# Row-tiled scores, joined latent weights and one shared order of work in a two-layer attention and feed-forward kernel

## The chip, the core and the metric

The kernel runs on one core of one Trainium2 chip. A core has TensorE (PE, matmuls), VectorE (DVE), ScalarE (ACT), GpSimd (POOL) and a queue for transfers (SP). Each engine takes its own instructions strictly in the order in which they are written, and semaphores join the engines. The metric is the device time of one execution in microseconds (us).

## The reference

Thirty-two entries of 128 tokens by 128 channels pass through two layers, each an attention and a feed-forward part, in float32:

```python
x = x + L0_xattn(ctx, layernorm(x), keep_mask, ...)   # 8 heads of 64, keys = context (120) and x (128)
x = x + L0_ffn(layernorm(x), Wm, Wp, Wc1, Wc2)        # iterated with a routed mask
x = x + L1_xattn(layernorm(x), ctx, ctx, mask, ...)   # 16 heads of 8, keys = context (120)
x = x + L1_ffn(layernorm(x), ...)                     # latent attention (16 heads of 8), then 8 experts
```

In the first attention q and k are divided by their own norms, the masked softmax runs over 248 keys, and the projected result is layer-normalized before it is added to x. In the latent attention of the last part the keys and values come from a narrow product:

```python
c = h @ Wdkv                     # 128 x 64
k = (c @ Wuk).reshape(B, S, HEADS, hd)
v = (c @ Wuv).reshape(B, S, HEADS, hd)
```

## The kernel before

x stays in the core's memory (SBUF) for the whole program. The stages run one after another, with a barrier between them: `l0_attention`, `l0_ffn` with `route`, `attention16` for L1 (names with `l_`), `attention16` for the latent attention (`mla_`), and `moe`.

**First attention.** The order of each engine is written out by hand in its `body(n)`, one entry n per turn, in `run_entries`; work of entry n+1 and n+2 is mixed in. Two units u of four heads each share the softmax. For entry n+2 the chain is: `norm_inputs` (DVE, L650, L652), `turn_inputs` (PE), `make_kvT` (ACT), three projections q, kc and kl (PE, L481, L482, L487) with their copies `qk` (ACT), squares `sq` (ACT, L591), `sum_squares` (DVE, L657 and L662 into `ssm`), and on POOL `norm_qk`: a power on 24 columns into `r_norm` (L742) and a product on 1536 columns into `qkn` (L745). In the next turn PE turns `qkn` (L494, L498, L504), ACT and DVE copy it to `KT` and `QZ`, and `scores` follows. A head has 64 rows of q; `QZ` holds each head's q in its own half of 128 rows with zeros in the other half, so that a score matmul (L384) uses all 128 rows. The key mask is added by a bfloat16 matmul per bank (L380). Softmax: `dve_max` (L162), exponentials (ACT, L171), `invert_sums` (DVE: L177, then L414 which copies the inverses wide into `r_wide`), transposes of the probabilities (L184, L190), their copies (ACT L196, DVE L201), `turn_sums` (L421), `multiply_v` (L436, L438), `scale_out` (L447) and `project` (L453). `y_moments` (L675 to L687) takes six small DVE instructions from the statistics of the projected row to its variance; POOL raises it to a power (L751), DVE normalizes (L692), POOL weighs and adds to x.

**The two 16-head attentions** have an order each (`body_l1`, `body_mla`), in turns by `run_steps`. PE writes the masks (L1431, 32 by 32 tiles) and the scores (L1436, four row tiles of 32) of an entry into four banks; DVE takes two maxima (L1558, L1565), the first for half the heads that ACT exponentiates with a bias (L1524), the second for the half that DVE shifts (L1574) and ACT exponentiates at once (L1531). Four groups of transposed probabilities (L1446) are copied by ACT or DVE (L1380) and multiplied with V and with ones in column tiles (L1456, L1459). The latent attention first projects to 64 columns (L1405), copies that on ACT (L1510), and takes keys and values from it (L1418, L1419).

## Time and profile before

| What | us |
|---|---|
| median of 3 runs (1519.94 to 1520.65) | 1520.29 |
| the profiled execution itself | 1520.62 |
| its span, first to last instruction | 1518.9 |
| PE busy | 1320.3 (87%) |
| DVE busy | 1031.7 (68%) |
| ACT busy | 759.3 (50%) |
| POOL busy | 559.6 (37%) |

The span is the time from the first to the last instruction of the program; some 1.7 us lie around it. In that execution the first attention works from 26 to 579 us, the first feed-forward part and its routing to 744, the L1 attention to 1010, the latent attention from 1042 to 1268, and the experts from 1277 to the end. A matmul of float32 is recorded as two passes, so that a count of 2 in a row is one matmul; its end is modelled, and the distance from one start to the next tells more than its duration. "PEclk" is the clock of PE that was granted, as a share of 2.4 GHz.

A window's row gives its bounds and length, then for PE, its weight loads (PEld), DVE, ACT and POOL the busy time and the number of instructions, then PEclk and what the DMA engines did. A timeline's row gives start, duration, engine, line, operation, output and input, the tile in TensorE as rows*columns, the shape, the count, and in brackets the idle time before it and what ended it.

### The profile page before, as it was taken

Reading aid. Unit: us, or ns where it says so; the run is one execution under the profiler, and the core shown is the slowest. Engines: PE = TensorE matmul, PEld = TensorE weight load, DVE = VectorE, ACT = ScalarE, POOL = GpSimd, SP = SyncE. Lnnn points to the kernel's source line nnn. Section 1 sums busy time; section 2 is a strip of 40 time slices with the busy share of each in tenths; the row PEclk is TensorE's granted clock in tenths of the full one; section 3 lists DMA queues with packets and bytes.
Section 4 is the critical chain, followed back from the end, with each engine's and each line's share of the span. In section 5 each row is a group of like instructions: output and inputs, shape, how many; then the busy total and the mean of one; then the engine's idle time right before and its main releaser. Section 6 shows DMA issues by size and latency. Waiting matters only on the chain. (4 is left out here: it accounts for less than half of the span.)

```text
span 1518.9 us, 38140 instructions
## 1 busy us (share of the span) xinstructions
PE 1320.3 (87%) x13781; PEld 963.8 (63%) x13781; DVE 1031.7 (68%) x2266; ACT 759.3 (50%) x2067; POOL 559.6 (37%) x546
## 2 busy tenths in 40 slices
PE   1699999999999996931389988969999997999998
PEld 0377676776776773421277676747878885777776
DVE  5377777777777773767388888868999995343432
ACT  1467767767767661300155555536666663333332
POOL 3556555555555543000221222234222222334333
PEclk9899999999999997965599999988999998999999
DMA  7000000000000000000000000010000000000000
GB/s 200 0 1 0 0 0 0 0 0 0 0 0 0 0 1 0 0 1 0 9 11 7 8 8 8 7 57 2 1 0 0 0 2 1 8 8 14 7 7 14
DMA packets 22727, 14.56 MB, mean 10 GB/s; under 512 B 6377, under 2 KB 21609, under 8 KB 22538
## 3 DMA queue, kind: packets, MB, share of 16 engines
q1 hardware_dynamic: 22520, 13.75, 3.5%
q8 instruction: 37, 0.61, 0.2%
q14 instruction: 24, 0.20, 0.0%
q10 hardware_dynamic: 146, 0.01, 0.0%
HBM read 11.66 MB, written 2.10 MB: 9 GB/s over the span
## 5 line engine op out<-in xcount | busy, mean ns | idle before, releaser
L742 POOL TENSOR_TENSOR r_norm<-ssm,mhalf 128x24 f32<-128x24 f32 x32 | 133.6, 4176 | 176.1 <-DVE ssm L662 176.1
L171 ACT ACTIVATE l_probs<-psum,l_n_max 128x248 f32<-128x248 f32 x256 | 117.0, 481 | 101.4 <-DVE l_n_max L162 101.4
L1845 ACT ACTIVATE hid<-psum 128x512 f32<-128x512 f32 x128 | 76.3, 597 | 136.3 <-PE psum L1793 136.3
L1906 DVE TENSOR_TENSOR prod<-psum,combine 128x512 f32<-128x512 f32 x64 | 44.2, 691 | 143.9 <-PE psum L1803 143.9
L1803 PEld LDWEIGHTS psum<-w,hid 128*128 128x128 f32 x1024 | 123.1, 192 | 26.8 <-issue 26.8
L1937 POOL TENSOR_TENSOR acc<-acc,prod 128x512 f32<-128x512 f32 x64 | 81.1, 1268 | 146.9 <-DVE prod L1906 146.9
L384 PE MATMUL psum<-KT,QZ 128*128 128x248 f32 x512 | 128.4, 373 | 0.0
L1803 PE MATMUL psum<-w,hid 128*128 128x128 f32 x1024 | 123.4, 275 | 0.0
L1793 PE MATMUL psum<-moe_hT,w 128*128 128x512 f32 x256 | 122.0, 605 | 0.0
L384 PEld LDWEIGHTS psum<-KT,QZ 128*128 128x128 f32 x512 | 98.1, 192 | 18.9 <-issue 0.7
L1658 POOL TENSOR_TENSOR l_QX<-l_qT,l_own_slots 128x512 f32<-128x512 f32 x32 | 33.3, 1040 | 185.1 <-ACT l_qT L1504 178.5
L745 POOL TENSOR_TENSOR qkn<-qk,r_norm 128x1536 f32<-128x1536 f32 x32 | 88.4, 2762 | 3.6 <-POOL r_norm L742 2.2
L1658 POOL TENSOR_TENSOR mla_QX<-mla_qT,mla_own_slots 128x512 f32<-128x512 f32 x32 | 33.3, 1040 | 149.5 <-ACT mla_qT L1504 149.5
L1380 ACT COPY l_probsT<-psum 120x512 f32<-120x512 f32 x64 | 37.5, 585 | 100.4 <-PE psum L1446 100.4
L162 DVE TENSOR_REDUCE l_n_max<-psum 128x4 f32<-128x992 f32 x64 | 75.7, 1183 | 8.8 <-PE psum L384 8.8
L1446 PE MATMUL psum<-ident,mla_probs 128*128 128x128 f32 x512 | 76.2, 283 | 1.5 <-ACT mla_probs L1524 1.3
L657 DVE TENSOR_REDUCE ss<-sq 128x24 f32<-128x1536 f32 x32 | 56.1, 1753 | 30.1 <-ACT sq L591 30.1
L1524 ACT ACTIVATE mla_probs<-psum,mla_n_max 128x128 f32<-128x128 f32 x256 | 69.5, 382 | 13.9 <-DVE mla_n_max L1558 13.9
L201 DVE COPY l_probsT<-psum 128x512 f32<-128x512 f32 x64 | 43.9, 685 | 41.6 <-PE psum L190 41.6
L1446 PE MATMUL psum<-ident,l_probs 128*120 128x128 f32 x512 | 70.5, 281 | 0.0
L1524 ACT ACTIVATE l_probs<-psum,l_n_max 128x120 f32<-128x120 f32 x256 | 68.0, 385 | 5.0 <-DVE l_n_max L1558 5.0
L586 ACT COPY qk<-psum 128x512 f32<-128x512 f32 (+1 forms) x96 | 54.5, 619 | 30.6 <-PE psum L487 22.7
(307 smaller groups left out, 3458.8 us busy)
## 6 DMA issues: line engine op xcount, KB each, us to landing
X<-x_in SPq DMA_DIRECT2D x8, 256.0 KB, 4.9
out_dram<-acc SPq DMA_DIRECT2D x32, 64.0 KB, 1.5
CT<-ctx_in SPq DMA_DIRECT2D x8, 240.0 KB, 6.2
l_cT<-ctxT_in SPq DMA_DIRECT2D x32, 60.0 KB, 1.8
w<-w_in SPq DMA_DIRECT2D x1, 1024.0 KB, 4.9
wm<-wm_in SPq DMA_DIRECT2D x1, 768.0 KB, 4.6
wp<-wp_in SPq DMA_DIRECT2D x1, 768.0 KB, 6.7
wkv<-wkv_in SPq DMA_DIRECT2D x1, 512.0 KB, 5.1
```

What stands on the lines that cost most here:

```text
L162: dve.tensor_reduce(n_max[u][:, :].rearrange("p (c j) -> p c j", c=2), psum[:, 2 * u:2 * u + 2, 0:HB * K].rearrange("p c (j k) -> p c j k" ...
L171: e = act.activation(probs[u][:, h, :], psum[:, 2 * u + h // HB, (h % HB) * K:(h % HB + 1) * K], ACT.Exp, bias=n_max[u][:, h:h + 1], accum ...
L384: mm = pe.matmul(psum[:, 2 * u + c, j * K:(j + 1) * K], QZ[par][:, h, :], KT[par][:, h // 2, :], start=False, stop=True, skip_group_check= ...
L742: pool.tensor_tensor(r_norm[:, :], ssm[:, :], mhalf[:, 0:3 * H], ALU.pow).then_inc(s["norm_inverted"], 1)
L745: pool.tensor_tensor(qkn[:, :, :].rearrange("p a (h d) -> p (a h) d", d=HD), qk[:, :, :].rearrange("p a (h d) -> p (a h) d", d=HD), r_norm ...
L1446: tr = pe.transpose(psum[0:K, 4 + g % 2, j * P:(j + 1) * P], probs[par][:, 4 * g + j, :], ident[:, :])
L1524: e = act.activation(probs[par][:, h, :], psum[:, h // 4, (h % 4) * K:(h % 4 + 1) * K], ACT.Exp, bias=n_max[par][:, h:h + 1])
L1658: pool.tensor_tensor(QX[par][:, :, :], qT[:, :].unsqueeze(1).broadcast_to([P, 4, P]), own_slots[:, :].unsqueeze(2).broadcast_to([P, 4, P]) ...
L1793: pe.matmul(psum[:, 2 + i % BANKS, :], w1[:, e, half * P:(half + 1) * P], hT[par][:, :], start=True, stop=True).then_inc(hidden[i], 1)
L1803: mm = pe.matmul(psum[:, 5 + e % 2, b * D:(b + 1) * D], hid[i % RING][:, b * P:(b + 1) * P], w2[:, i, :], start=(half == 0), stop=(half == ...
L1845: act.activation(hid[i % RING][:, :], psum[:, 2 + i % BANKS, :], ACT.Silu).then_inc(activated[i], 1)
L1937: pool.tensor_tensor(a[:, :, :], a[:, :, :], prod[e % 2][:, :, :], ALU.add).then_inc(summed[e], 1)
```

## The change

It has four parts.

1. **Row tiles in the first attention.** `QT` holds q without zeros, two heads in the two halves of 128 rows. A score matmul takes 64 rows, and the two heads of a pair stand next to each other in the order, each with its own bank. The mask is added by matmuls of 64 rows likewise, from `keep_now`, which POOL copies for each entry; the mask row is made twice at the start, in rows 0 and 64. `multiply_v` alternates between its two column tiles.
2. **Aggregate moments.** `bn_aggr` and one addition replace the six instructions between `y_stat` and `y_var`.
3. **Joined latent weights.** Once, at the start of the latent attention, PE forms Wdkv Wuk and Wdkv Wuv (`joined`). Keys and values then come straight from `zT`; L1405, the copy L1510 and the waits on it go.
4. **Orders.** The first attention gets a new order on every engine and now uses `run_steps`, which also does its first and last entries. Both 16-head attentions share one new `body` on every engine.

```diff
+        joined = sb("joined", [D, 2, D])
+                    pe.transpose(psum[0:LAT, 6, 0:D], wdkv[:, :], ident[:, :]).then_inc(w_turned, 1)
+                    pe.wait_ge(w_copied, 1)
+                    pe.matmul(psum[:, 7, 0:D], wdkvT[:, :], wk[:, :], start=True, stop=True)
+                    pe.matmul(psum[:, 7, D:2 * D], wdkvT[:, :], wv[:, :], start=True, stop=True).then_inc(w_joined, 1)
...
-            pe.matmul(psum[:, 2 * u + c, 0:2 * K], first_row[:, :], keep_row[:, entries(n), :].broadcast_to([P, 2, K]),
-                      start=True, stop=False, skip_group_check=True)
-            for j in range(2):
-                h = 4 * u + 2 * c + j
-                mm = pe.matmul(psum[:, 2 * u + c, j * K:(j + 1) * K], QZ[par][:, h, :], KT[par][:, h // 2, :],
-                               start=False, stop=True, skip_group_check=True)
+                        for r in range(2):
+                            pe.matmul(psum[:, 2 * u + r, 0:2 * K], first_row[64 * r:64 * r + 64, :],
+                                      keep_now[par][64 * r:64 * r + 64, :].unsqueeze(1).broadcast_to([64, 2, K]),
+                                      start=True, stop=False, skip_group_check=True)
+                        for j in range(2):
+                            for r in range(2):
+                                mm = pe.matmul(psum[:, 2 * u + r, j * K:(j + 1) * K], QT[par][64 * r:64 * r + 64, 2 * u + j, :],
+                                               KT[par][64 * r:64 * r + 64, 2 * u + j, :], start=False, stop=True,
+                                               skip_group_check=True)
...
+                for r in (0, 64):
+                    dve.tensor_scalar(keep_row[r:r + 1, :, 0:C], keep8[r:r + 1, :].rearrange("a (b c) -> a b c", b=B), 1.0, -NEG_MAX,
+                                      ALU.subtract, ALU.mult)
...
-                    dve.tensor_tensor(y_sums[:, :], y_stat[:, 1:3], y_stat[:, 4:6], ALU.add)
-                    dve.tensor_tensor(y_diff[:, :], y_stat[:, 1:2], y_stat[:, 4:5], ALU.subtract).then_inc(s["y_aggr"], 1)
...
+                        dve.bn_aggr(y_moment[:, :], y_stat[:, :]).then_inc(s["y_aggr"], 1)
+                        wait(dve, s["y_aggr"], n + 1)
+                        wait(dve, s["y_inverted"], n)
+                        dve.tensor_scalar(y_var[:, :], y_moment[:, 1:2], LN_EPS, None, ALU.add).then_inc(s["y_var_ready"], 1)
...
+                def body(n, par):
+                    values_x(n + 1)
+                    scores(n, 1, par)
+                    project(n - 1)
+                    turn_inputs(n + 2)
+                    turn_probs0(n, 0)
+                    turn_probs1(n, 0)
+                    project_kc(n + 2)
+                    turn_sums(n, 0)
+                    project_q(n + 2)
+                    multiply_v(n, 0, par)
+                    turn_probs0(n, 1)
+                    turn_kc(n + 1)
+                    project_kl(n + 2)
+                    turn_probs1(n, 1)
+                    turn_kl(n + 1)
+                    turn_q(n + 1)
+                    multiply_v(n, 1, par)
+                    turn_sums(n, 1)
+                    values_c(n + 2)
+                    scores(n + 1, 0, 1 - par)
...
+                def body(n, par):
+                    norm_inputs(n + 2)
+                    maximum(n, 1)
+                    invert_sums(n, 0)
+                    y_moments(n - 1)
+                    copy_pt1(n, 0)
+                    scale_out(n, 0)
+                    invert_sums(n, 1)
+                    copy_pt1(n, 1)
+                    copy_kl(n + 1, 1 - par)
+                    copy_qT(n + 1, 1 - par)
+                    sum_squares(n + 2)
+                    y_normalize(n - 1)
+                    maximum(n + 1, 0)
+                    scale_out(n, 1)
+                    x_moments(n - 2)
...
+                def body(n, par):
+                    weigh(n - 2)
+                    copy_keep(n + 2, par)
+                    invert_deviation(n - 1)
+                    add_to_x(n - 2)
+                    invert_norms(n + 2)
+                    norm_qk(n + 2)
+                    later_scales(n)
...
+                def body(n, par):
+                    copy_q(n + 1)
+                    copy_group(act.copy, act, n - 1, 2)
+                    copy_k(n + 1, 1 - par)
+                    exp_b(n, par)
+                    copy_group(act.copy, act, n, 0)
+                    exp_a(n + 1, 1 - par)
...
+                def body(n, par):
+                    copy_input(dve, n + 1)
+                    copy_group(dve.tensor_copy, dve, n - 1, 3)
+                    add_projection(n - 2)
+                    max_b(n, par)
+                    take_stats(n - 2)
+                    shift_b(n, par)
+                    copy_group(dve.tensor_copy, dve, n, 1)
+                    copy_values(dve.tensor_copy, dve, n + 1, 1 - par)
+                    invert_sums(n - 1)
+                    scale_out(n - 1)
+                    max_a(n + 1, 1 - par)
```

The first place is DVE in a turn of the first attention. Before, from the wide copy of the inverses for unit 0 (`r_wide0`) to the scaled output; `l0_n_max1` is the maximum of unit 1:

```order
L177 RECIPROCAL l0_r_sums0<-l0_sums0 128x4
L414 COPY r_wide0<-l0_r_sums0 128x256
L162 TENSOR_REDUCE l0_n_max1<-psum 128x4
L201 COPY l0_probsT0<-psum 128x512
L675 BN_STATS y_stat<-y 128x6
L678 TENSOR_TENSOR y_sums<-y_stat 128x2
L679 TENSOR_TENSOR y_diff<-y_stat 128x1
L681 TENSOR_SCALAR y_mean<-y_sums 128x1
L682 TENSOR_SCALAR y_within<-y_sums 128x1
L683 SCALAR_TENSOR_TENSOR y_between<-y_diff 128x1
L687 TENSOR_TENSOR y_var<-y_within,y_between 128x1
L447 TENSOR_TENSOR outT<-psum,r_spread 128x256
```

The same place after the change:

```order
L577 TENSOR_SCALAR ln_c<-CT,mean_c,rstd_c 120x128
L607 TENSOR_REDUCE l_n_max1<-psum 128x4
L615 RECIPROCAL l_r_sums0<-l_sums0 128x4
L618 COPY r_wide0<-l_r_sums0 128x256
L640 BN_STATS y_stat<-y 128x6
L642 BN_AGGR y_moment<-y_stat 128x2
L645 TENSOR_SCALAR y_var<-y_moment 128x1
L626 COPY l_probsT0<-psum 128x512
L634 TENSOR_TENSOR outT<-psum,r_spread 128x256
```

The maximum now stands ahead of the wide copy, and the moments of y ahead of the copy of the probabilities instead of behind it.

The second place is PE in the first attention, from the end of `multiply_v` of unit 1 to `project` (L453 before, L444 after). Before:

```order
L380 MATMUL psum<-keep_row,first_row 128x496
L384 MATMUL psum<-KT,QZ 128x248 x2
L380 MATMUL psum<-keep_row,first_row 128x496
L384 MATMUL psum<-KT,QZ 128x248 x2
L380 MATMUL psum<-keep_row,first_row 128x496
L384 MATMUL psum<-KT,QZ 128x248 x2
L380 MATMUL psum<-keep_row,first_row 128x496
L384 MATMUL psum<-KT,QZ 128x248 x2
L453 MATMUL psum<-wo,outT 128x128 x4
```

After:

```order
L420 MATMUL psum<-ident,r_wide 128x128 x2
L368 MATMUL psum<-wkv,kvT 120x512
L386 MATMUL psum<-keep_now,first_row 128x496 x2
L391 MATMUL psum<-KT,QT 128x248 x4
L375 MATMUL psum<-wkv,kvT 128x512
L386 MATMUL psum<-keep_now,first_row 128x496 x2
L391 MATMUL psum<-KT,QT 128x248 x4
L444 MATMUL psum<-wo,outT 128x128 x4
```

The number of score and mask matmuls is the same (eight and four); the two value projections now stand ahead of each unit's scores.

The third place is PE in the L1 attention, one turn. Before, from one `project` (L1466) to the next transposes (L1446):

```order
L1466 MATMUL psum<-l_wo,l_outT 128x128
L1431 MATMUL psum<-l_bias,ident_bf 32x480 x16
L1436 MATMUL psum<-l_kT,l_QX 128x120 x16
L1446 MATMUL psum<-ident,l_probs 120x128 x8
L1456 MATMUL psum<-l_probsT,l_V 32x128 x4
L1459 MATMUL psum<-l_probsT,l_ONE 32x128 x4
L1456 MATMUL psum<-l_probsT,l_V 32x128 x4
L1459 MATMUL psum<-l_probsT,l_ONE 32x128 x4
L1399 MATMUL psum<-ident,l_zn 128x128
L1406 MATMUL psum<-l_zT,l_wq 128x128
L1418 MATMUL psum<-l_cT,l_wk 128x120
L1419 MATMUL psum<-l_wv,l_cT 120x128
```

After, from the scores (L1386) to the second half of V (L1406):

```order
L1386 MATMUL psum<-l_kT,l_QX 128x120 x16
L1396 MATMUL psum<-ident,l_probs 120x128 x8
L1358 MATMUL psum<-ident,l_zn 128x128
L1416 MATMUL psum<-l_wo,l_outT 128x128
L1396 MATMUL psum<-ident,l_probs 120x128 x4
L1365 MATMUL psum<-l_zT,l_wq 128x128
L1367 MATMUL psum<-l_cT,l_wk 128x120
L1368 MATMUL psum<-l_wv,l_cT 120x128
L1406 MATMUL psum<-l_probsT,l_V 32x128 x4
L1409 MATMUL psum<-l_probsT,l_ONE 32x128 x4
L1406 MATMUL psum<-l_probsT,l_V 32x128 x4
L1409 MATMUL psum<-l_probsT,l_ONE 32x128 x4
```

The input's transpose is now separated from the projection that needs its copy by eight to twelve other passes, `project` is a turn later, and the groups of transposes lie between other work.

## Rows read from the trace of the kernel before

**Rows 1.** Windows: one turn each of the first, the L1 and the latent attention.

```profile
324.10:340.30 16.20, 16.18 (x106) 11.48 (x105) 11.99 (x26) 11.21 (x32) 8.88 (x7) 1.00 0.00 0
861.20:869.20 8.00, 7.15 (x138) 5.58 (x138) 6.66 (x12) 4.54 (x13) 1.80 (x3) 1.00 0.03 8
1137.20:1144.60 7.40, 7.40 (x147) 5.90 (x141) 6.92 (x10) 4.74 (x16) 2.19 (x4) 1.00 0.00 0
```

**Rows 2.** Timeline of PE in a turn of the first attention: start, duration, instruction.

```profile
324.98 1.02 PE L462 MATMUL psum<-wkv,kvT 128*120 128x512 f32 x2
325.84 0.60 PE L184 MATMUL psum<-ident,l_probs 128*120 128x128 f32 x4
326.27 0.60 PE L190 MATMUL psum<-ident,l_probs 128*128 128x128 f32 x4
...
335.00 0.45 PE L436 MATMUL psum<-l_probsT,VC 120*64 120x128 f32 x4
...
336.08 0.38 PE L380 MATMUL psum<-keep_row,first_row 128*128 x1
336.30 1.00 PE L384 MATMUL psum<-KT,QZ 128*128 128x248 f32 x4
337.14 0.37 PE L380 MATMUL psum<-keep_row,first_row 128*128 x1
```

**Rows 3.** Timeline of PE in a turn of the L1 attention, then of the latent attention.

```profile
861.49 0.42 PE L1431 MATMUL psum<-l_bias,ident_bf 32*32 32x480 bf16 x16
...
862.94 1.09 PE L1446 MATMUL psum<-ident,l_probs 128*120 128x128 f32 x8
863.96 0.43 PE L1456 MATMUL psum<-l_probsT,l_V 120*32 120x128 f32 x8
...
864.97 0.33 PE L1399 MATMUL psum<-ident,l_zn 128*128 128x128 f32 x1
...
1138.73 0.43 PE L1405 MATMUL psum<-mla_zT,mla_wdkv 128*64 128x128 f32 x2
1139.10 0.49 PE L1406 MATMUL psum<-mla_zT,mla_wq 128*128 128x128 f32 x2
...
1141.40 0.66 PE L1446 MATMUL psum<-ident,mla_probs 128*128 128x128 f32 x4
1141.99 0.48 PE L1418 MATMUL psum<-mla_latT,mla_wk 64*128 64x128 f32 x2
```

**Rows 4.** Timeline of DVE in the first attention, second half of the same turn.

```profile
333.26 0.69 DVE L201 COPY l_probsT<-psum 128x512 f32<-128x512 f32 x1 [1.33 <-PE psum L190]
334.15 0.76 DVE L372 TENSOR_SCALAR QZ<-psum,qk_scale 64x512 f32<-64x512 f32 x1 [0.21 <-PE psum L498]
...
336.59 1.75 DVE L657 TENSOR_REDUCE ss<-sq 128x24 f32<-128x1536 f32 x1 [0.47 <-ACT sq L591]
338.38 0.18 DVE L662 TENSOR_SCALAR ssm<-ss 128x24 f32<-128x24 f32 x1
338.46 1.18 DVE L162 TENSOR_REDUCE l_n_max<-psum 128x4 f32<-128x992 f32 x1
```

**Rows 5.** Timelines of POOL and of DVE: what stood beside `qkn`.

```profile
322.45 4.18 POOL L742 TENSOR_TENSOR r_norm<-ssm,mhalf 128x24 f32<-128x24 f32 x1 [5.00 <-DVE ssm L662]
326.79 2.76 POOL L745 TENSOR_TENSOR qkn<-qk,r_norm 128x1536 f32<-128x1536 f32 x1 [0.16 <-POOL r_norm L742]
...
338.63 4.17 POOL L742 TENSOR_TENSOR r_norm<-ssm,mhalf 128x24 f32<-128x24 f32 x1 [5.00 <-DVE ssm L662]
...
327.87 1.69 DVE L678 TENSOR_TENSOR y_sums<-y_stat 128x2 f32<-128x2 f32 x1
...
69.28 2.76 POOL L745 TENSOR_TENSOR qkn<-qk,r_norm 128x1536 f32<-128x1536 f32 x1
...
69.40 2.79 DVE L414 COPY r_wide<-l_r_sums 128x256 f32<-128x256 f32 x1
```

**Rows 6.** Timeline of DVE ahead of the first attention.

```profile
21.13 2.14 DVE L331 TENSOR_SCALAR keep_row<-keep 1x3840 bf16<-1x3840 uint8 x1
```

More of the change, by code:

```diff
@@ L206, in run_entries, with run_steps @@
-def run_entries(eng, body, before_loop=None):
-    body(0, 0, first=True)
-    if before_loop:
-        before_loop()
-    with eng.Fori(0, B // 2 - 2) as i:
-        body(2 * i + 1, 1)
-        body(2 * i + 2, 0)
-    body(B - 3, 1)
-    body(B - 2, 0, after=False)
-    body(B - 1, 1, after=False, next_=False)
+def run_steps(eng, body):
+    for n in range(-2, 4):
+        body(n, n % 2)
+    with eng.Fori(0, B // 2 - 4) as i:
+        body(2 * i + 4, 0)
+        body(2 * i + 5, 1)
+    for n in range(B - 4, B + 2):
+        body(n, n % 2)
@@ L458, in _, with turn_inputs, project_kc @@
             def _(pe):
+                def turn_inputs(m):
+                    if there(m):
+                        wait(pe, s["ln_made"], m + 1)
+                        wait(pe, s["vc_copied"], m)
+                        pe.transpose(psum[:, 6, 0:C], ln_c[0:C, :], ident[0:C, 0:C])
+                        pe.transpose(psum[:, 6, P:2 * P], ln_x[:, :], ident[:, :]).then_inc(s["ln_turned"], 1)
+                def project_kc(m):
+                    if there(m):
+                        wait(pe, s["kvT_made"], m + 1)
+                        pe.matmul(psum[0:C, 6, :], kvT[:, 0:C], wkv[:, 0:INNER], start=True, stop=True).then_inc(s["kc_proj"], 1)
@@ L459, in values_c, with turn_kl @@
+                def turn_kl(m):
+                    if there(m):
+                        wait(pe, s["kcT_copied"], m + 1)
+                        for c in range(4):
+                            tr = pe.transpose(psum[:, 6, c * P:(c + 1) * P], qkn[:, 2, c * P:(c + 1) * P], ident[:, :])
+                        tr.then_inc(s["klT_turned"], 1)
                 def values_c(m):
-                    wait(pe, s["klT_copied"], m)
-                    pe.matmul(psum[0:C, 6, :], kvT[:, 0:C], wkv[:, INNER:], start=True, stop=True).then_inc(s["vc_proj"], 1)
+                    if there(m):
+                        wait(pe, s["klT_copied"], m)
+                        wait(pe, s["kc_copied"], m + 1)
+                        pe.matmul(psum[0:C, 6, :], kvT[:, 0:C], wkv[:, INNER:], start=True, stop=True).then_inc(s["vc_proj"], 1)
@@ new lines, in project @@
+                def project(n):
+                    if there(n):
+                        wait(pe, out_scaled[1], n + 1)
+                        for c in range(4):
+                            mm = pe.matmul(psum[:, 5, 0:D], outT[:, c, :], wo[:, c, :], start=(c == 0), stop=(c == 3))
+                        mm.then_inc(s["projected"], 1)
+                def body(n, par):
[19 more added lines that the diff above has]
+                    scores(n + 1, 0, 1 - par)
@@ L561, in _ @@
+                run_steps(pe, body)
             @block.scalar
@@ L585, in copy_qk, with copy_part @@
+                def copy_part(m, part, proj, copied, bank, rows):
+                    if there(m):
+                        wait(act, s["normed"], m)
                         wait(act, s[proj], m + 1)
-                        act.copy(qk[0:rows, i, :], psum[0:rows, bank, :]).then_inc(s[copied], 1)
+                        act.copy(qk[0:rows, part, :], psum[0:rows, bank, :]).then_inc(s[copied], 1)
                 def square_qk(m):
-                    wait(act, s["kl_copied"], m + 1)
-                    wait(act, s["ss_summed"], m)
```

827 lines of the change are left out of this document (329 added, 498 removed).

## The prediction

> **What bounds the kernel now.** I read the time spent by stage first, then the windows of one turn, then the timelines of PE, DVE and POOL within a turn. The reader should see in the windows that PE is busy in 16.18 of 16.20 us of a turn of the first attention, at the full clock, with DVE at 11.99, ACT at 11.21 and POOL at 8.88 [rows 1]. So the first attention, 553 of the 1518.9 us (26 to 579), is bound by PE, and what is taken from PE counts until another chain is longer. In the L1 attention PE has 7.15 of 8.00 us and DVE 6.66, and no engine is full: there the order sets the turn. The latent attention has PE at 7.40 of 7.40 and DVE at 6.92 [rows 1]; PE first, and DVE closely behind.
>
> From start to start PE needs 0.86 us for a matmul of 512 columns in its two passes, 0.43 to 0.44 for four transposes (0.109 each), 0.84 for four score passes of 248 columns (0.21 each), 0.22 for the mask of a bank, and 1.08 for `multiply_v` of a unit, from its first L436 to the mask behind it [rows 2].
>
> **First attention on PE.** Before, eight heads take 16 score passes and four masks: 16 × 0.21 + 4 × 0.22 = 4.2 us. After, a score matmul uses 64 rows, and two heads stand in the two halves of the array with separate banks. If the halves work side by side, eight pairs of passes remain, 8 × 0.209 = 1.67, and two pairs of masks, 2 × 0.21: 2.09. If they do not, the 4.2 stay. No row of this stage has two row tiles; in the L1 attention the 16 masks and 16 score matmuls of four row tiles take 1.45 us together (861.49 to 862.94 [rows 3]), while 32 score passes one after another would alone be 32 × 0.109 = 3.5, so row tiles with their own banks do run side by side. I take 2.09.
>
> The turn after, by PE's order: `project` 8 passes at 0.109, 0.87; `turn_inputs` 0.22; transposes of probabilities 4 × 0.44 = 1.75; five products of 512 columns, 4.30; `turn_sums` of both units, four transposes, 0.44; twelve transposes of `qkn`, four of them narrower, 1.29; `multiply_v` 2 × (1.08 + 0.10 to enter its tiles) = 2.36; scores 2.09. The new order also has four more changes of tile shape than the old, one into and one out of each unit's 64-row scores. A change costs what the eight L1 transposes show ahead of V's 32-column tiles: 1.02 instead of 8 × 0.109 = 0.87, so 0.15 [rows 3]; four are 0.60. Sum 13.92. The same sum for the kernel before is 13.92 − 2.09 − 0.60 + 4.2 = 15.43, and its turn, from one start of L742 to the next, is 338.63 − 322.45 = 16.18 [rows 5], so 0.75 us are waits. Those waits can't be read one by one, since busy PE covers them. The two value projections (0.86 each) now fill the time in which a copy is waited for, so I take 0.45, with 0.2 and 0.8 as ends: **14.37 us a turn** (14.1 to 14.7). Over 30 full turns the gain is 1.81 × 30 = 54 us.
>
> The Trainium skill, "TensorEngine Tiling (Array Packing)", section "Key Properties", says that a change of tiling mode drains TensorE, while different tiles run in parallel. The first half speaks against this change; if four drains cost nothing the turn would be 13.8, and at 0.15 they are in the sum. The L1 rows agree with both halves.
>
> Outside the 30 turns the first attention has 553 − 30 × 16.18 = 68 us. `run_steps` now does the first and last entries too, and entry 1's inputs are turned while entry 0 is still waited for. At most one turn's worth of work comes beside other work (18), at least none: I take 9.
>
> **The small edits of the first attention.** The mask row is made twice: 2.14 us more on DVE ahead of the stage [rows 6]; POOL is filling its own constants beside it, so I take 0.6 (0 to 2.14). The second DMA of the mask lies beside the first. `keep_now` is one small copy on POOL, which is busy 8.88 of 16.20 us [rows 1]; it stands behind the weighing and ahead of the power, so its 0.4 to 0.6 us come out of POOL's wait of 5.00 us for `ssm` [rows 5] as long as it is issued before `ssm`: nothing. The zeroing of `QZ` goes, off the path. The six moment instructions become three; DVE has 4.2 us to spare in a turn, so this is worth nothing by itself, but see below.
>
> **L1 attention.** PE's order after: scores 1.45, eight transposes 0.87, the input 0.11, `project` 0.22, four transposes 0.44, q, k and values 0.66 + 0.15 for the shape, half of V 1.01, transposes with a shape change 0.59, half of V 1.01 [rows 3]: 6.51. DVE loses nothing of size; its 6.66 of busy time [rows 1] is the floor. A little waiting at each shape change gives 6.85 (6.7 to 7.2). The reason why the 8.00 of before should fall: the input's transpose, its copy and the projection that needs it stood in a row on PE, and now other transposes lie between them. (8.00 − 6.85) × 30 = 34.5.
>
> **Latent attention.** L1405 goes, 0.37 from its start to L1406's. Ahead of the 64-row latent products four transposes took 1141.40 to 1141.99, 0.59 instead of 0.44, so a shape change of 0.15 goes, and another ahead of L1406 [rows 3]; 0.37 + 0.30 = 0.67 off PE. The wait of PE on ACT's copy of the latent rows goes as well. 7.40 − 0.67 = 6.73, and DVE's 6.92 [rows 1] stands just above it: its work changes by one copy of 512 columns less (0.61, as L201's 0.69 less 0.08 of overlap [rows 4]) and two small copies more, about 6.7. I take 6.95 (6.7 to 7.2): 0.45 × 30 = 13.5. Forming `joined` at the start (three small matmuls and two copies) lies beside the loads and DVE's own preparation: 0 (0 to 2).
>
> **Sum.** 54 + 9 + 34.5 + 13.5 − 0.6 = 110.4. Against the profiled execution, 1520.62 (span 1518.9 and 1.7 around it), that gives **1410 us**; the median 1520.29 differs by 0.3.
>
> **What is late next in the first attention.** When PE gives back 1.8 us, the chain through `qkn` has to fit too. `qkn` runs 2.76 us on POOL and DVE may be held for all of it: beside it L414, the wide copy, ran 2.79 us, from 0.11 after its start to 0.15 after its end, and the small L678 1.69, ending with it [rows 5]. So a DVE instruction of these kinds must be through before `qkn` begins. Before, `r_wide0` went right behind `invert_sums`, well ahead. Now `maximum(n, 1)` stands ahead of it. Clock from unit 1's L190: L201 starts about 0.64 later, then three copies of 512 (0.61, 0.61, 0.68) and the sum of squares, 1.79 [rows 4], so `ssm` is there at 4.32, `r_norm` starts at 4.57, and `qkn` 4.34 behind it (326.79 − 322.45 [rows 5]) at 8.91, to 11.67. PE from the same moment: L190 0.44, `turn_kl` and `turn_q` 0.87, `multiply_v` with its entry to 2.5, `turn_sums` 2.76 to 2.98, values 3.62, scores of unit 0, then of the next turn values to 5.83 and scores of unit 1, landed at 7.22; its maximum 1.10 [rows 4] to 8.32, the inverse to 8.53, and the wide copy can start at about 8.57. The margin is 0.3 us. I take it that it holds, because `qkn` itself can't come earlier than that chain, but this is the weakest place of the forecast.
>
> **Rivals.**
> A, the forecast: 1410, margin holds and the moments don't lie beside `qkn`'s lock.
> B, the variance is held. `y_moments` now stands behind `r_wide0`, at 8.9 and later, right where `qkn` runs. L678 was held there for 1.69 instead of about 0.2 us [rows 5], but it reads two inputs; whether `bn_aggr` and the one-element addition of L645 are held no row shows. For: L414, with one input, was. Against: an instruction of one element. If held to 11.67, `copy_pt1(n, 0)` waits behind it, and with it `multiply_v` of unit 0: from 11.67 the copy 0.7, multiply_v 1.2, and the rest of the turn: about 15.4, a loss of 1.03 × 30 = 31 against A, and 4 more at the ends: 1445. The Trainium skill, "SBUF — State Buffer", section "Who interferes with whom", gives the single rule that only the shared port pair contends and "it's an exclusive lock", for DVE's fast forms and two-input forms. By it the addition could be held, and the time would be B's; the rows for L414 and L678 agree, and the rest is open.
> C, `r_wide0` is late by the 0.3 us and is held to 11.70. Then 0.32 + 0.2 + 0.11 for the moments, 0.72 for the copy, 1.2, and the transposes and products behind it, 16.1 in all: the first attention gains nothing. 1520.6 − 48 − 6 = 1466. For: 0.3 us is less than the error of my waits, and the loop feeds itself, since a held turn moves scores and `qkn` alike. Against: a longer turn also delays `sq` and `ssm`, which moves `qkn` back.
> E, the order of both 16-head attentions brings nothing: 1410 + 48 = 1458. For: DVE's 6.66 and 6.92 leave little, and PE's shape changes may add. Against: PE's own idle 0.85 in L1.
> R, the change does not do what it says: the row tiles do not run side by side. PE's sum is 13.92 + 2.1 + waits = 16.5: 1520.6 + 10 − 57 = 1473. Against: the L1 row.
> D, slower. If C holds PE idle for 1.5 us or more in each turn, the granted clock, 1.00 in all three windows [rows 1], may fall to 1.2 GHz for a part s of PE's work, which then takes twice as long: s × 14 us. 1466 + 30 × 14 s passes 1520.3 from s = 0.13; at s = 0.3 it is 1592. For it: such idle stretches would be longer than any in a turn now. Against: no row shows a fall in this stage.
>
> **How the numbers follow.** A 0.44, B 0.21, C 0.19, E 0.07, R 0.04, D 0.05. The likeliest gives 1410, by its own ends 1396 to 1425. B and C reach to 1445 and 1466, with R at 1473; below 1396 and above 1473 lie some 0.12 together. Range 1396 to 1473. A measurement of this kernel tells 0.2%, 3 us, from no change. A, B, C, E and R, 0.95 together, are all faster; 0.02 of it may be eaten up by a lesser D that ends at no change: faster 0.93, same 0.02, slower 0.05.
>
> **What would show it.** The distance from one L444 to the next after it: 14.4 (A), 15.4 (B), 16.1 (C), 16.5 (R). The two L391 of a pair starting within a few ns of each other. The duration of L618 for unit 0: 0.3 in A, 2.8 in C; that of L645: 0.2 in A, 2 or more in B. L1386 coming every 6.85 us in L1 and 6.95 in the latent attention. The first L444 about 9 us earlier. PEclk at 1.00 throughout. The forecast is wrong if the first attention still takes over 480 us with L618 unheld, or the two others over 7.3 us a turn.

## The result and the profile after

The changed kernel takes 1404.65 us (median of 4 runs, 1403.03 to 1405.34), the kernel before 1520.39 us (1519.94 to 1520.65). The ratio is 0.9238, 95% interval 0.9222 to 0.9254. The forecast was 1410 us, range 1396 to 1473. The profiled execution has a span of 1403.6 us, 115.3 less than before.

A turn is one entry's round of an engine's loop, and its length is the distance from one `project` to the next. The two traces give these stretches; each ends with the start of the last pass of the last `project`, and the 16-head attentions begin with the first instruction of their preparation:

| Stretch | before | after | difference | forecast |
|---|---|---|---|---|
| start to the first `project` | 81.3 | 69.8 | -11.5 | -9 and +0.6 |
| first attention, first to last `project` | 493.6 | 440.4 | -53.2 | -54 |
| first feed-forward part and routing | 151.2 | 151.6 | +0.5 | 0 |
| pause between routing and L1 | 10.6 | 13.4 | +2.8 | 0 |
| L1 attention | 272.4 | 234.0 | -38.4 | -34.5 |
| latent attention, with the pause of 2.2 ahead | 257.6 | 241.9 | -15.7 | -13.5 |
| experts | 252.3 | 252.5 | +0.2 | 0 |

The windows of one turn of the three attentions after the change (bounds, length, busy time of PE, PEld, DVE, ACT and POOL, granted clock) answer to [rows 1]:

```profile
300.00:314.40 14.40, 14.38 (x108) 9.36 (x106) 10.11 (x22) 11.46 (x33) 9.11 (x8) 1.00 0.00 0
800.00:806.70 6.70, 6.70 (x140) 5.52 (x139) 6.55 (x13) 4.52 (x15) 1.80 (x3) 1.00 0.04 9
1100.00:1106.74 6.74, 6.74 (x139) 5.53 (x138) 6.69 (x12) 4.62 (x14) 2.16 (x4) 1.00 0.00 0
```

PE fills its turn in all three now, L1 included. From one L444 to the next it is 14.39 and 14.43 us in turn (14.37 forecast); from one L1386 to the next 6.69 in L1 (6.85 forecast) and 6.74 in the latent attention (6.95 forecast). The clock is 1.00 as before.

PE's timeline in the part of a turn that holds the scores, which answers to [rows 2]:

```profile
310.17 0.44 PE L420 MATMUL psum<-ident,r_wide 128*128 128x128 f32 x2
310.45 1.02 PE L368 MATMUL psum<-wkv,kvT 128*120 128x512 f32 x2
311.40 0.38 PE L386 MATMUL psum<-keep_now,first_row 64*128 64x496 bf16 x2
311.62 1.00 PE L391 MATMUL psum<-KT,QT 64*128 64x248 f32 x8
312.55 1.13 PE L375 MATMUL psum<-wkv,kvT 128*128 128x512 f32 x2
313.61 0.38 PE L386 MATMUL psum<-keep_now,first_row 64*128 64x496 bf16 x2
313.83 1.00 PE L391 MATMUL psum<-KT,QT 64*128 64x248 f32 x8
314.76 1.16 PE L444 MATMUL psum<-wo,outT 128*128 128x128 f32 x8
```

Eight score passes of 64 rows take 0.93 us from the first to the next instruction (311.62 to 312.55), where four passes of 128 rows took 0.84. One by one in the trace, the two passes of a pair start 3 to 4 ns apart and the pairs 0.21 us: the halves do run side by side. Ahead of the masks the product of 512 columns takes 0.95 instead of 0.86, and behind the scores 0.10 remains, so one unit's scores cost 1.15 plus 0.1 for entering; the forecast had 1.05 plus 0.30 for the two changes.

DVE and POOL at the place that the forecast called its weakest, which answers to [rows 5]:

```profile
301.59 0.17 DVE L615 RECIPROCAL l_r_sums<-l_sums 128x4 f32<-128x4 f32 x1
301.79 0.29 DVE L618 COPY r_wide<-l_r_sums 128x256 f32<-128x256 f32 x1
302.00 0.28 DVE L640 BATCH_NORM_STATS2 y_stat<-y 128x6 f32<-128x128 f32 x1
302.39 0.18 DVE L642 BATCH_NORM_AGGREGATE y_moment<-y_stat 128x2 f32<-128x6 f32 x1
302.61 0.15 DVE L645 TENSOR_SCALAR y_var<-y_moment 128x1 f32<-128x1 f32 x1
302.69 0.69 DVE L626 COPY l_probsT<-psum 128x512 f32<-128x512 f32 x1
```

```profile
302.28 2.76 POOL L691 TENSOR_TENSOR qkn<-qk,r_norm 128x1536 f32<-128x1536 f32 x1
```

The wide copy starts 0.49 us ahead of `qkn` (0.43 in every other turn) and runs free in 0.29 us. `bn_aggr` and the addition start while `qkn` runs, and take 0.18 and 0.15 us: they are not held, that is, they don't wait for its end. So case A came true at both places, and case B did not.

### The profile page after: what moved, and what is told of

Read it like the earlier page. It is cut to its first block and busy times, and to the rows that moved or that the text cites. A ratio compares the mean times of both kernels' runs of the same rounds, so it can differ in the third digit from the quotient of the medians.

```text
span 1403.6 us, 38151 instructions
## 1 busy us (share of the span) xinstructions
PE 1232.4 (88%) x13722; PEld 882.8 (63%) x13722; DVE 964.3 (69%) x2172; ACT 764.4 (54%) x2005; POOL 568.8 (41%) x582
## 5 line engine op out<-in xcount | busy, mean ns | idle before, releaser
L634 DVE TENSOR_TENSOR outT<-psum,r_spread 128x256 f32<-128x256 f32 x64 | 26.9, 420 | 78.8 <-PE psum L435 73.3
L1396 PE MATMUL psum<-ident,l_probs 128*120 128x128 f32 x512 | 76.6, 283 | 0.8 <-ACT l_probs L1453 0.5
L1692 PEld LDWEIGHTS psum<-moe_hT,w 128*128 128x128 f32 x256 | 45.3, 195 | 35.9 <-issue 35.4
L1339 ACT COPY mla_probsT<-psum 128x512 f32<-128x512 f32 x64 | 39.3, 614 | 48.7 <-PE psum L1396 48.7
```

What stands on the lines that cost most here:

```text
L1339: copy(probsT[0:K, g, :, :], psum[0:K, 4 + g % 2, :].rearrange("k (j q) -> k j q", j=4)).then_inc(copied[g], 1)
L1396: tr = pe.transpose(psum[0:K, 4 + g % 2, j * P:(j + 1) * P], probs[par][:, 4 * g + j, :], ident[:, :])
L1692: pe.matmul(psum[:, 2 + i % BANKS, :], w1[:, e, half * P:(half + 1) * P], hT[par][:, :], start=True, stop=True).then_inc(hidden[i], 1)
```

## The experiments

The first eight ask what the first attention owes to which part. But for the last two kernels of this section, each was run once; what is read from a single run is read from its turns, which repeat some thirty times in a trace. The kernel before took 1521.47 us (one run) beside the six moments, the late wide copy, the full rows and the row tiles alone, and 1520.76 us (1519.14 to 1523.89) beside the small filler, the eased old order, the joined weights alone and the later powers.

**The six moments at the new place.**

```diff
-                        dve.bn_aggr(y_moment[:, :], y_stat[:, :]).then_inc(s["y_aggr"], 1)
+                        dve.tensor_tensor(y_sums[:, :], y_stat[:, 1:3], y_stat[:, 4:6], ALU.add)
+                        dve.tensor_tensor(y_diff[:, :], y_stat[:, 1:2], y_stat[:, 4:5], ALU.subtract).then_inc(s["y_aggr"], 1)
...
```

> The changed kernel with the six small moment instructions of before in place of bn_aggr and the addition, at the new place (behind the wide copy of unit 0, ahead of the copy of its probabilities). There they begin 0.1 us after qkn has started (302.39 against 302.28). Theory: the two-input ones are held to the end of qkn (L678 was held 1.69 us before), so the first takes about 2.6 us, the copy of the probabilities starts near 306 instead of 302.7, multiply_v of unit 0 starts 1.7 us later, and the turn of the first attention goes from 14.41 to about 15.9 us: 1450 us. Rival: the 1.35 us between that copy and multiply_v hide most of it, or the loop shifts qkn back: turn under 14.8 us, under 1417 us.

Measured: 1457.64 us, turn 16.10 and 16.13 in alternation. DVE and POOL in one turn of this kernel:

```profile
312.79 0.29 DVE L622 COPY r_wide<-l_r_sums 128x256 f32<-128x256 f32 x1
...
313.22 2.76 POOL L701 TENSOR_TENSOR qkn<-qk,r_norm 128x1536 f32<-128x1536 f32 x1
...
313.39 2.60 DVE L646 TENSOR_TENSOR y_sums<-y_stat 128x2 f32<-128x2 f32 x1
315.92 0.15 DVE L647 TENSOR_TENSOR y_diff<-y_stat 128x1 f32<-128x1 f32 x1
...
317.44 0.44 PE L439 MATMUL psum<-l_probsT,VC 120*64 120x128 f32 x4 [1.67 <-issue]
```

An addition of two elements takes 2.60 us, because it starts 0.17 us behind `qkn`; the last row is PE's `multiply_v`, ahead of which PE stands still for 1.67 us. The turn is longer by that time (14.41 + 1.67 = 16.08). So `bn_aggr` is worth 52 us in this order (1457.64 less the 1405.34 of the changed kernel's profiled run), though it saves DVE only a few small instructions.

**The wide copy late.**

```diff
                     maximum(n, 1)
+                    filler(n)
                     invert_sums(n, 0)
...
+                        dve.bn_stats(spare[:, :], wo[:, :, :].rearrange("p c d -> p (c d)"))
```

> The changed kernel with one more DVE instruction (statistics over 512 constant columns, some 0.6 us, nobody reads them) between the maximum of unit 1 and the inverse of unit 0. The wide copy of unit 0 started 0.5 us ahead of qkn; now it would start 0.1 us or more behind qkn's start. Theory (my case C): it is held to the end of qkn, 2.8 us, turn_sums and with it the q projection on PE come 1.5 us later, turn about 16 us: 1453 us. Rival: only the 0.6 us of more DVE work count, or nothing, since DVE has 4 us to spare in a turn: turn 14.4 to 15.0, 1405 to 1423 us.

Measured: 1459.54 us, turn 16.18 and 16.31 in alternation:

```profile
314.59 0.69 DVE L614 BATCH_NORM_STATS2 spare<-wo 128x6 f32<-128x512 f32 x1
...
315.19 2.76 POOL L697 TENSOR_TENSOR qkn<-qk,r_norm 128x1536 f32<-128x1536 f32 x1
...
315.39 2.71 DVE L623 COPY r_wide<-l_r_sums 128x256 f32<-128x256 f32 x1
```

The copy now starts 0.20 us behind `qkn` and takes 2.71 us; in every other turn it starts 0.11 behind and takes 2.80. This is case C, forecast at 16.1 us a turn.

**The same with 128 columns.**

```diff
-                        dve.bn_stats(spare[:, :], wo[:, :, :].rearrange("p c d -> p (c d)"))
+                        dve.bn_stats(spare[:, :], wo[:, 0, :])
```

> As the run with the late wide copy, but the added DVE instruction covers 128 columns instead of 512 (some 0.2 us instead of 0.6). The wide copy of unit 0 starts 0.49 us ahead of qkn in the changed kernel, so 0.29 us stay. Theory of a threshold: nothing happens, turn of the first attention 14.4 us, 1404 us. Rival: DVE's added time counts in proportion (0.6 us cost 1.8 us a turn, so 0.2 us cost 0.6): turn 15.0 us, 1422 us.

Measured: 1402.73 us, turn 14.39 and 14.43. The wide copy starts at 301.82, `qkn` at 302.25; in the next turn the copy starts at 316.30 and `qkn` at 316.51, only 0.2 us behind it. It takes 0.29 us both times, although `qkn` begins before the second one ends: what counts is which of the two starts first. So it is a threshold: 0.2 us more of DVE work cost nothing, 0.6 us cost some 55 us. (That the time is 2 us below the changed kernel's belongs to the pause ahead of L1, below.)

**Full rows in the new order.**

```diff
-QT[par][64 * r:64 * r + 64, 2 * u + j, :], KT[par][64 * r:64 * r + 64, 2 * u + j, :]
+QZ[par][:, 2 * (2 * u + j) + r, :], KT[par][:, 2 * u + j, :]
```

> The changed kernel with the score matmuls and masks on all 128 rows again (QZ with zeros, as before), in the new order of everything. Theory: PE loses what the row tiles gave, 4.19 instead of 2.29 us of masks and scores and 0.2 to 0.4 us less for tile shape changes: turn 14.41 + 1.9 - 0.3 = 16.0 us, 1453 us; the new order by itself gives 0.2 us a turn. Rival: the new order removes waits that the row tiles only cover: turn 15.5 us or less, under 1438 us.

Measured: 1463.21 us, turn 16.18 and 16.31. By my theory's number (16.0) this fits PE's own length, but the trace has something else beside it:

```profile
300.84 1.19 DVE L608 TENSOR_REDUCE l_n_max<-psum 128x4 f32<-128x992 f32 x1 [0.73 <-PE psum L392]
...
300.96 2.76 POOL L692 TENSOR_TENSOR qkn<-qk,r_norm 128x1536 f32<-128x1536 f32 x1
...
302.15 1.73 DVE L619 COPY r_wide<-l_r_sums 128x256 f32<-128x256 f32 x1
```

With longer scores the maximum of unit 1 comes later against `qkn`, and the wide copy is held for 1.73 us. By the distances of its row starts PE loses only some 0.3 us to it. So most of the 1.8 us is PE's own time. With the hold the new order and the aggregate gain nothing over the old turn of 16.18; without it the turn would be some 15.9, by my estimate (16.24 less 0.3).

**Row tiles alone, in the old order.** The kernel before with `QT`, 64-row scores and masks, `keep_now` and the second mask row.

> The kernel before with the row tiles alone: 64-row scores and masks in pairs, the per-entry mask copy on POOL, the mask row made twice; orders, six moment instructions and the 16-head attentions as before. Theory: the first attention was bound by PE, so the turn falls by 1.9 less the changes of tile shape, to 14.6 us: 1520 - 47 = 1473 us. Rival: in the old order a chain besides PE ends last as soon as PE is shorter (L678 held by qkn, or both maxima waiting behind both scores): the turn stays at 15.3 us or more, 1494 us or more, and the new order is needed for the gain.

Measured: 1516.77 us, turn 16.06. The rival was right, and my theory and my forecast's sum for this part were not. Scores and masks shrink from 4.19 to 2.09 us, and all of PE's work in a turn from 16.18 to 14.45, close to the 14.41 of the changed kernel; the turn shrinks by 0.12. The timelines of PE, DVE and ACT show what stands in their place:

```profile
302.13 1.75 DVE L681 TENSOR_REDUCE ss<-sq 128x24 f32<-128x1536 f32 x1 [0.47 <-ACT sq L615]
...
302.94 1.01 PE L391 MATMUL psum<-KT,QT 64*128 64x248 f32 x8
...
303.92 0.18 DVE L686 TENSOR_SCALAR ssm<-ss 128x24 f32<-128x24 f32 x1
304.00 1.18 DVE L162 TENSOR_REDUCE l_n_max<-psum 128x4 f32<-128x992 f32 x1
305.10 0.41 DVE L472 TENSOR_TENSOR outT<-psum,r_spread 128x256 f32<-128x256 f32 x1
...
305.22 0.47 ACT L171 ACTIVATE l_probs<-psum,l_n_max 128x248 f32<-128x248 f32 x1 [3.13 <-DVE l_n_max L162]
...
305.57 0.60 PE L478 MATMUL psum<-wo,outT 128*128 128x128 f32 x3 [1.61 <-DVE outT L472]
```

The scores are done by 304, but `outT`, which `project` needs, stands behind the sum of squares and a maximum on DVE. The 4.2 us of old scores had just covered that. In the kernel before, at the end of the turn of [rows 4]:

```profile
339.56 0.41 DVE L447 TENSOR_TENSOR outT<-psum,r_spread 128x256 f32<-128x256 f32 x1
340.27 0.94 PE L453 MATMUL psum<-wo,outT 128*128 128x128 f32 x7
```

There `outT` is done at 339.98, 0.30 us ahead of `project`. With row tiles alone it is done at 305.52, 0.06 ahead. So DVE's queue had 0.24 us to spare, and no more than that could be gained. 0.10 of it went to `project`, whose passes take 0.99 us behind 64-row tiles instead of 0.89.

**The old order eased.**

```diff
+                    scale_out(dve, n, 1)
                     if next_:
                         t["dve_max"](dve, n + 1, 0)
+                    if after:
+                        sum_squares(n + 2)
```

> The kernel before with the row tiles alone, and in DVE's old order two moves: the scaled output of unit 1 and then the maximum of unit 0 ahead of the sum of squares instead of behind it. With row tiles alone PE stood still for 1.61 us ahead of project, because DVE took the sum of squares (from 302.13) and the maximum before it scaled the output. Theory: that queue on DVE is what ended last; turn 16.06 to about 15.0 us, 1517 - 32 = 1485 us, not 14.4, since the maximum of unit 1 and its exponentials still follow both scores. Rival: the sum of squares is late now and qkn with it, the transposes of qkn wait in its place: turn 15.8 us or more.

Measured: 1536.06 us, turn 16.59 to 16.68, slower than before. My theory fell; the rival's mechanism was right, and its floor of 15.8 us is passed by 0.8. PE no longer waits ahead of `project`, but 1.47 us elsewhere:

```profile
303.85 2.76 POOL L767 TENSOR_TENSOR qkn<-qk,r_norm 128x1536 f32<-128x1536 f32 x1 [0.16 <-POOL r_norm L764]
...
305.15 1.61 DVE L436 COPY r_wide<-l_r_sums 128x256 f32<-128x256 f32 x1
...
306.64 1.07 ACT L610 COPY qk<-psum 128x512 f32<-128x512 f32 x2 [1.74 <-POOL qkn L767]
...
307.28 1.12 PE L512 MATMUL psum<-wkv,kvT 128*128 128x512 f32 x2 [1.47 <-ACT qk L610]
```

The sum of squares came late, `qkn` with it, and `qkn` has two ways to be late: ACT may not overwrite `qk` before it ends, and now unit 1's wide copy is held too.

**The aggregate alone, and row tiles with the aggregate**, both in the old order.

> The kernel before with bn_aggr and one addition in place of the six small instructions, at their old place and nothing else. Theory: the 1.69 us for which L678 was held disappear, but PE was busy through the whole turn, so the turn stays at 16.18 us and the time at 1520 us. Rival: the held L678 delayed the scaled output of unit 0 and with it PE: turn 15.8 us or less, 1509 us or less.

> The kernel before with the row tiles and with bn_aggr, in the old order: parts 1 and 2 of the change without part 4. With row tiles alone the turn was 16.06 us. Theory: what ends last there is the queue on DVE of sum of squares, maximum of unit 0, scaled output of unit 1, which the moments don't touch: 16.06 us stay, 1517 us, so the new order is needed. Rival: the hold of L678 (1.53 us there) is what keeps the loop at 16 us: turn 14.6 to 15.2 us, 1475 to 1493 us.

Measured: 1522.53 us with turn 16.18, and 1513.79 us with turn 16.05, beside 1521.07 (1519.11 to 1522.58) for the kernel before. In the first, `bn_aggr` and the addition at the old place take 0.18 and 0.15 us, none of them held, and the turn hasn't moved by 0.01 us. Both theories held. The turns of the first attention together (the times of those in the new order also have the gains of the other two attentions):

| row tiles | aggregate | new order | turn | time |
|---|---|---|---|---|
| no | no | no | 16.18 | 1520.39 |
| no | yes | no | 16.18 | 1522.53 |
| yes | no | no | 16.06 | 1516.77 |
| yes | yes | no | 16.05 | 1513.79 |
| no | yes | yes | 16.24 | 1463.21 |
| yes | no | yes | 16.11 | 1457.64 |
| yes | yes | yes | 14.41 | 1404.65 |

No two of the three parts give more than 0.13 us of the 1.77; each is needed. The new order with neither of the others was not tried, nor which of its moves it takes.

**Joined weights alone, in the old order.** The kernel before with `joined`; L1405 and the copy L1510 are gone, the products of 64 rows are products of 128.

> The kernel before with the joined latent weights alone, in the old order of both 16-head attentions (PE still waits for the copy of q before it takes keys and values). Theory: PE bound the latent attention, and 0.37 us of L1405 and 0.30 us of tile shape changes go: turn 7.35 to 6.75 us, 1521 - 18 = 1503 us, so that the new order adds nothing there. Rival: the old order hangs on DVE and ACT as well (DVE was busy 6.92 of 7.40 us): turn 7.1 us or more, 1513 us or more, and the new order is what brings 6.74.

Measured: 1506.04 us; the latent turn is 6.91 us. Between theory (6.75) and rival (7.1): of the 0.61 us a turn, the joined weights give 0.44 and the order 0.17. The window of one turn there:

```profile
1150.08:1156.98 6.90, 6.73 (x140) 5.56 (x138) 6.83 (x11) 4.58 (x14) 2.15 (x4) 1.00 0.00 0
```

PE has 0.17 us of idle, and DVE is busy for 6.83 of 6.90. Over the whole stage that kernel takes 240.4 us against 239.8 with the new order: what the order gives in 28 turns it nearly loses in the first ones.

**The powers on POOL later.** Most of that loss is on POOL. In the changed kernel the latent attention starts thus:

```profile
916.89 1.48 POOL L119 TENSOR_TENSOR rstd<-small,mhalf 128x7 f32<-128x7 f32 x1 [2.01 <-POOLq L1222]
918.34 1.48 POOL L119 TENSOR_TENSOR mla_scale<-small,mhalf 128x7 f32<-128x7 f32 x1
919.79 0.40 POOL L1545 TENSOR_TENSOR mla_centred<-X,mean 128x128 f32<-128x128 f32 x1
...
920.62 0.40 POOL L1552 TENSOR_TENSOR mla_zn<-mla_centred,mla_scale 128x128 f32<-128x128 f32 x1
924.03 1.04 POOL L1565 TENSOR_TENSOR mla_QX<-mla_qT,mla_own_slots 128x512 f32<-128x512 f32 x1 [3.02 <-ACT mla_qT L1440]
```

The shared `body` centres entry n + 1 where the old ones centred n + 2, so that two powers for later entries now stand ahead of the first entry.

```diff
-                    if isinstance(n, int) and n < 2:
-                        some = slice(FIRST + 7 * (n + 2), FIRST + 7 * (n + 3))
+                    if isinstance(n, int) and 0 <= n < 4:
+                        some = slice(FIRST + 7 * n, FIRST + 7 * (n + 1))
```

> The changed kernel with the powers for later entries on POOL put two turns later in both 16-head attentions (later_scales from n = 0 instead of n = -2). In the changed kernel they stand ahead of the first entry's centring: 1.5 us in L1 (680.73 to 682.19) and 3.0 us in the latent attention (916.89 to 919.8), and again ahead of the second and third entries. Theory: the first input is turned 1.5 and 3.0 us earlier and the first turns of the latent attention (8.1, 8.2 and 7.7 us) come nearer to 7.4: 4 to 6 us less, 1399 to 1401 us. Rival: the powers now stand in front of a spread of q in a running turn instead and cost the same there (1.5 us in L1 and 3 us in the latent attention, four times): no gain, 1404 us or more.

Measured: 1402.14 us (1401.21 to 1402.92), ratio to before 0.9218 (0.9202 to 0.9233), which overlaps that of the changed kernel. The stages gain 0.8 and 1.4 us. The start is early as expected, but the third to fifth latent turns take 7.4, 7.3 and 8.2 us, where the changed kernel had 7.8 and then 6.74: mostly the rival.

**The powers behind the input.**

```diff
                     norm_input(n + 1)
+                    later_scales(n)
                     spread_q(n + 1, 1 - par)
-                    later_scales(n)
```

> The changed kernel, with the powers for later entries on POOL behind norm_input and ahead of spread_q, from n = -1 on, where POOL waits 3.0 us for q in the first turns (921.02 to 924.03), and with the 0.2 us DVE instruction of the run with the small filler. Theory: the powers fit into that wait, so L1 starts 1.5 us earlier and its second turn takes 6.7 instead of 8.05 us; the latent attention starts 3.0 us earlier and its first turns lose 1.4, 1.4 and 1.0 us; together 9.7 us in the two stages. And the pause between routing and L1 is 11.05 us as with the small filler, not 13.44 as in the changed kernel (there DVE's branch takes 2.4 us, which goes with where DVE's code lies): 2.4 us. 1404.65 - 12 = 1392.5 us, 1390 to 1396. Rival 1: the spread of q waits for the powers and only half is gained: 1397 to 1400 us. Rival 2: the pause is a matter of chance: 2.4 us more.

Measured: 1398.73 us (1395.56 to 1399.12), ratio to before 0.9196 (0.9183 to 0.9208), which lies below that of the changed kernel: the best version. It is rival 1's range, and the theory's 1392.5 was too low. In the trace the latent stage gains 4.4 us (235.4), L1 0.8 (233.1), the pause 1.7 (11.7). This is the fastest of the five executions; 1.5 us more lie in the first feed-forward part and 0.8 ahead of the first `project`, which the edit doesn't aim at. Its POOL at the start of the latent attention:

```profile
912.82 0.40 POOL L1558 TENSOR_TENSOR mla_zn<-mla_centred,mla_scale 128x128 f32<-128x128 f32 x1
913.17 1.48 POOL L119 TENSOR_TENSOR rstd<-small,mhalf 128x7 f32<-128x7 f32 x1
914.62 1.48 POOL L119 TENSOR_TENSOR mla_scale<-small,mhalf 128x7 f32<-128x7 f32 x1
916.23 1.04 POOL L1571 TENSOR_TENSOR mla_QX<-mla_qT,mla_own_slots 128x512 f32<-128x512 f32 x1
```

Two powers fit into the wait for q almost exactly. The second turns still take 8.55 us in L1 and 8.49 in the latent attention, so 9.7 us was too much to expect. The windows of these two turns and of the third latent one, from scores to scores, show why:

```profile
689.71:698.26 8.55, 8.55 (x150) 7.36 (x136) 5.18 (x8) 4.47 (x13) 4.03 (x6) 0.72 0.04 9
925.51:934.00 8.49, 8.49 (x150) 7.26 (x136) 5.41 (x8) 4.34 (x13) 5.72 (x9) 0.73 0.01 2
934.00:940.74 6.74, 6.74 (x153) 5.53 (x138) 6.70 (x12) 4.48 (x14) 4.40 (x5) 1.00 0.01 2
```

PE is busy for the whole of the second turns, at a mean granted clock of 0.72 and 0.73. In the first latent turn the clock is 0.50 and PE is busy 5.83 of 7.55 us; from the third on it is 1.00. So the second turns are held by PE's own clock, and POOL has nothing to give there. In the changed kernel they took 8.05 and 8.11 us at 0.81 and 0.80.

## Why the prediction was right, point by point

**PE's sum in the first attention.** Total 14.37 forecast, 14.41 measured, partly by terms that cancel. By row starts `project` took 1.00 (0.87), the five products of 512 columns 4.84 (4.30), the transposes of `qkn` 1.52 (1.29), those of the probabilities 1.98 (1.75): 1.1 us more than summed. `multiply_v` took 2.06 instead of 2.36, scores 2.30 instead of 2.09, and the 0.60 for shape changes and the 0.45 for waits are contained in those longer starts. In the same way the waits of before that I took as 0.75 were largely such longer starts, which is why the difference of the two sums held better than their parts. That the parts cancel so well is luck.

**Side by side.** Right; R fell. The pairs start 3 to 4 ns apart.

**What is late next.** The mechanism, a wide copy 0.3 us ahead of `qkn`, was right, and the size was 0.49 and 0.43. The sum itself had a slip: the value projection of unit 0 is put at 3.62 us, though `turn_sums` ends at 2.98 and the projection takes 0.86; with 3.84 the margin would have been 0.1. That it came out larger is luck. The two runs with an added instruction put the edge between 0.2 and 0.6 us of added work: a copy that starts 0.2 us ahead of `qkn` is free, one that starts 0.1 behind is held. They put the price at 1.8 us a turn, as case C said. This was the true risk of the change: some 54 of 115 us hung on 0.5 us.

**B, the held variance.** Wrong in kind for the new instructions and right for the old ones. The Trainium skill, "SBUF — State Buffer", section "Who interferes with whom", names two-input forms and DVE's fast forms as what contends; the traces agree: beside `qkn` a two-input addition of two elements took 2.60 us (six moments) and the wide copy 2.71 (late wide copy), while `bn_aggr` and the addition of one element took 0.18 and 0.15 (changed kernel). I had named the addition as open and put 0.21 on it. I also priced a hold there at 15.4 us a turn; held, it was 16.1, because PE's wait of 1.67 us ahead of `multiply_v` counts in full, and I had let 1.03 of it count.

**The step that failed: the gain of the first attention as PE's time alone.** The text gave all 54 us to the row tiles, with the order only as a risk. Row tiles alone bring 0.12 us a turn. That PE was busy for the whole turn said that nothing else was longer, not how far behind the next chain was: it was 0.24 us behind. The trace of before showed it: the sum of squares, its 1.79 us, and the maximum of unit 0 stood on DVE beside the scores [rows 4], and `outT` behind them, done 0.30 us ahead of `project`. I had asked what comes next in the new order only, and there the answer was right. The total came out because the change had the order with it, and not for the reason that the sum gave.

**L1.** 6.69 against 6.85: the 0.34 of waits that I added to PE's 6.51 were 0.18. PE fills the turn, DVE has 6.55 of 6.70. Between the input's transpose and the projection that needs it lie six passes in the trace (0.96 us), not eight to twelve. E fell: in L1 nothing but the order changed, and it gave 1.3 us a turn.

**Latent attention.** 6.74 against 6.95. The turn before was 7.35 by its `project` rows; my 7.40 was the length of the window. DVE's busy time came out as summed (6.7), and PE ran as long as DVE. But the start of the stage costs 3.3 us more than before (from the first instruction of its preparation to the first input's transpose 9.7 against 6.4 us), 3.0 of it for the two powers on POOL. The prediction had no term for it; the text ahead of it lets the stage begin at 1042 us, where the trace has its first instruction at 1011.3. Forming `joined` was hidden: its last copy ends at 913.8, DVE's preparation at 916.6.

**Start.** 11.5 us earlier instead of 8.4, inside the ends of 0 and 18. **D** did not come: the clock stayed 1.00 in the turns, and also in those of the kernels whose PE waited 1.6 us a turn (1.00 from 300 to 332 us with six moments, with the late wide copy and with row tiles alone). That no row shows a fall in this stage was too much said: in the kernel before the clock is 0.85 from 26 to 82 us, where PE is busy 36.4 of 56 us.

**The pause ahead of L1**, 2.8 us longer, had no step.

## What to carry to other kernels

A fully busy engine bounds the kernel only until its work shrinks; before work is taken from it, ask for each instruction that waits for it what else stands in front of that instruction on its own engine. If a long GpSimd product holds DVE's two-input and wide instructions, the order on DVE has an edge: a few tenths of a microsecond decide over the whole length of that product, so look at the starts of the two, and swap small two-input operations there for forms that a trace shows unheld, as `bn_aggr` here; one input alone is no safe sign, since the wide copy has one and was held. When a shared order shifts an index by one, look at the first turns on every engine, and at PE's clock in them, not at the loop alone.

## What the runs showed of the hardware

The pause between the routing and L1, in which no engine computes, differs with code that runs elsewhere. It is 10.6 to 10.8 us in the old order with and without row tiles (11.45 with `bn_aggr` alone), 13.4 in the changed kernel and in the one with later powers, and 14.0 with full rows; with one DVE instruction more in the first attention it is 11.3 and 11.05, with six moments 11.2. From a conditional branch of DVE's sequencer to its next instruction 0.6 to 3.0 us pass there, and not at the same branches in all kernels: 2.4 us for one 2.4 us into the pause in the changed kernel, 2.75 us for one at 4.3 us in the kernel before. These two nearly cancel: 9.6 us into the pause in the changed kernel, and 9.5 in the kernel before, DVE has its branches behind it and waits for the others. The 2.8 us between the two kernels are on PE's sequencer, whose last conditional branch takes 3.61 us in the changed kernel and 0.62 in the kernel before:

```profile
L834 PEldq COMPARE_BRANCH  x1: 3606/3606/3606, 670.5 to 670.5; - x1
L876 PEldq COMPARE_BRANCH  x1: 617/617/617, 734.6 to 734.6; - x1
```

With the small filler PE's last branch takes 3.42 us and DVE's long one is gone (0.7), which makes the pause 11.05; in the last kernel, with the same filler, PE's takes 4.01 and the pause 11.7. That this goes with where the code lies in memory is a guess that no run tested by itself; eight packets of the instruction queues move in the pause in both kernels.

After such pauses PE's clock is low: in the changed kernel it is 0.50 from 921.0 to 933.9 us, 0.80 in the next turn, and 1.00 from 942 on. The 32 score passes of a latent entry take 2.02 us from the first to the next instruction at 933.90, and 1.10 at 1104.85, where the clock is 1.00.

A two-input DVE instruction that started 0.17 us after the GpSimd product was held to its end, although it has two elements only: 2.60 us. In the eased old order it comes ahead of the product and takes 0.16.
